# A message-passing layer on one core: the node half of the update moved from the node stage to the end of each group, eight early chunks in place of ten, and early gathers gated on finished table groups

## The reference

```
h   = relu(layernorm(x))                                  # 12500 x 128
m   = relu(concat(h[src], edge_attr) @ msg_w1 + msg_b1)   # 400000 x 128, edge_attr 400000 x 64
msg = m @ msg_w2 + msg_b2
agg = segment_sum(msg, dst)                               # 12500 x 128
u   = relu(concat(h, agg) @ upd_w1 + upd_b1)
out = x + u @ upd_w2 + upd_b2
```

## Time and profile before

| what | value |
|---|---|
| median of three runs | 4690.09 us |
| the profiled execution | 4662.54 us, span 4660.7 us |
| busy: PE, PE weight loads | 2531.2 us, 2175.3 us |
| busy: POOL, DVE, ACT | 2953.8 us, 1924.0 us, 130.3 us |
| granted PE clock, mean | 0.686 of 2.4 GHz |
| HBM | 340.79 MB of packets, 73 GB/s |

### The profile page before, as it was taken

How to read it: one execution, slowest core, us unless ns; L and a number is a source line. 1 busy time by engine, 2 the same in 40 slices (tenths; PEclk the granted TensorE clock), 3 DMA queues, 4 the chain that set the end, 5 groups by cost and what they waited for, 6 DMA issues and landing times.

```text
span 4660.7 us, 32266 instructions
## 1 busy us (share of the span) xinstructions
PE 2531.2 (54%) x10696; PEld 2175.3 (47%) x10696; DVE 1924.0 (41%) x1990; ACT 130.3 (3%) x257; POOL 2953.8 (63%) x3133
## 2 busy tenths in 40 slices
PE   1756555555545555555555455555555555544655
PEld 1655444454444444444444444544444444444554
DVE  1745434344343343443443433434434334344534
ACT  1520000000000000000000000000000000000000
POOL 6265566666666666666666666666666666665665
PEclk6877766666676666666676767667666666666766
DMA  4322222222222222222222222222222222233322
GB/s 112 125 71 73 67 67 72 67 67 72 67 66 72 67 70 68 67 72 67 67 72 67 66 72 67 72 67 67 72 67 66 72 67 70 80 94 86 90 77 59
DMA packets 154626, 340.79 MB, mean 73 GB/s; under 512 B 73895, under 2 KB 74919, under 8 KB 154187
## 3 DMA queue, kind: packets, MB, share of 16 engines
q0 software_dynamic: 100000, 205.00, 16.8%
q1 hardware_dynamic: 46165, 121.97, 8.1%
q10 hardware_dynamic: 8406, 13.14, 0.9%
HBM read 327.06 MB, written 12.81 MB: 73 GB/s over the span
## 4 chain that ended last, share of the span: by engine, by line
issue 40%; PE 24%; POOL 19%; DVE 8%; another core or an unknown queue 6%; DMA 3%; DVEq 0%; ACT 0%; SPq 0%; POOLq 0%
POOL rows L403 19%; PE pre L487 11%; PE seg L540 9%; DVE rows L967 4%; DMA rows<-table,index 3%; DVE h_space L1021 2%; PE seg L458 1%; PE spare L555 1%; PE spare L556 1%; DVE space L1007 0%; PE pre L462 0%; PE spare L585 0%; DVEq L1046 0%; PE pre L508 0%
## 5 line engine op out<-in xcount | busy, mean ns | idle before, releaser
L403 POOL DMA_INDIRECT rows<-table,index x3045 | 2877.1, 945 | 1661.9 <-issue 1091.2
L487 PE MATMUL pre<-w_attr_sb,attrs 128*128 128x256 f32 x3126 | 1339.5, 599 | 1379.6 <-issue 967.4
L487 PEld LDWEIGHTS pre<-w_attr_sb,attrs 128*128 128x128 f32 x3126 | 907.0, 304 | 1663.3 <-issue 1042.2
L967 DVE TENSOR_TENSOR rows<-pre,rows 128x1024 f32<-128x1024 f32 x381 | 465.9, 1223 | 2318.4 <-DMA rows<-table,index 2215.4
L540 PE MATMUL seg<-space,rows 128*128 128x80 f32 x6250 | 965.8, 306 | 547.8 <-issue 547.0
L540 PEld LDWEIGHTS seg<-space,rows 128*128 128x128 f32 x6250 | 988.7, 232 | 560.1 <-issue 513.3
L1087 DVE TENSOR_TENSOR rows<-rows,iota_ps 128x1024 f32<-128x1024 f32 x381 | 464.7, 1220 | 13.1
L1021 DVE TENSOR_REDUCE h_space<-space 128x240 f32<-128x1920 f32 x130 | 438.4, 3373 | 0.0
L1007 DVE TENSOR_TENSOR space<-iota_ps,dst_rel 128x1920 f32<-128x1920 f32 x131 | 280.8, 2144 | 7.3 <-issue 5.9
L787 ACT ACTIVATE h_space<-update 128x500 f32<-128x500 f32 x25 | 27.5, 1101 | 4315.0 <-DVEq L1090 4160.5
L555 PE MATMUL spare<-h_space,w_msg_t_sb 128*128 128x240 f32 (+1 forms) x262 | 112.7, 524 | 6.5 <-issue 4.1
(11 more groups left out here) (77 smaller groups left out, 456.0 us busy)
## 6 DMA issues: line engine op xcount, KB each, us to landing
attrs<-in_attr SPq DMA_DIRECT2D x130, 768.0 KB
rows<-table,index POOLq DMA_INDIRECT x3045
table<-rows SPq DMA_DIRECT2D x20, 224.0 KB
h_space<-in_x ACTq DMA_DIRECT2D x13, 224.0 KB
out<-h_space ACTq DMA_DIRECT2D x13, 224.0 KB
table_first<-in_x ACTq DMA_DIRECT2D x12, 224.0 KB
out<-table_first ACTq DMA_DIRECT2D x12, 224.0 KB
x_all<-in_x SPq DMA_DIRECT2D x2, 1120.0 KB
```

The source lines that it names most:

```text
L403: pool.indirect_dma_start(slot_rows(j)[:, t, :], None, source, bass.IndirectOffsetOnAxis(index[0:EDGES, j, t:t + 1], 0))\
L487: return pe.matmul(columns(j, q, PAIR)[:, two * 2 * D:(two + 1) * 2 * D], attrs[:, j % 2, start:start + EDGES], w_attr_sb[:, :], start=Tru ...
L967: dve.tensor_tensor(hidden, columns(j, q, tiles), hidden, ALU.add).then_inc(summed, 1)
```

## The change

The node half leaves the node stage. `update` is set to zero by ACT instead, in five copies of 2500 columns after its last group. When a group is finished, PE multiplies the group's transposed `h` by `w_node`, adds the group's part of `update` by a product with the identity, both into PSUM, and ACT's relu reads that with the bias. Two early chunks fewer are gathered from `x`, and five of the eight wait for table groups: chunk 3 for group 1, then 5, 9, 12 and 16. The entries of `FIRST_LEADS` are the same.

```diff
-EARLY = 3
-EARLY_CHUNKS = 10
+EARLY = 2
+EARLY_CHUNKS = 8
+
+EARLY_GATES = {3: 1, 4: 5, 5: 9, 6: 12, 7: 16}
...
             for s in range(EARLY_CHUNKS):
                 j, q = divmod(s, PAIRS)
+                if s in EARLY_GATES:
+
+                    pool.wait_ge(table_made, after(EARLY_GATES[s]))
                 gather(x, j, range(q * PAIR, (q + 1) * PAIR))
...
                 last.then_inc(table_ready, 1)
-                pe.wait_ge(update_made, after(g, BACK[k]))
-                pe.matmul(pre[:, k % 2, 512:512 + GROUP], w_node_sb[:, :], h_group(g),
-                          start=True, stop=True).then_inc(update_ready, 1)
...
             def finish_group(g):

+                pe.wait_ge(updates_in, g + 1)
+                need(pe, o_made, g)
+                pe.matmul(spare[:, 0:GROUP], w_node_sb[:, :], h_group(g), start=True, stop=False)
+                pe.matmul(spare[:, 0:GROUP], identity[:, :], update[:, g * GROUP:(g + 1) * GROUP], start=False, stop=True).then_inc(u_summed, 1)
+
                 pe.wait_ge(u_relued, g + 1)
-                need(pe, o_made, g)
...
-            def update_out(g, k):
-
-                act.wait_ge(update_ready, after(g))
-                act.sem_inc(act_turns, 1)
-                act.activation(update[:, bass.ds(g * GROUP, GROUP)], pre[:, k % 2, 512:512 + GROUP], ACT.Identity,
-                               bias=b_upd1_col[:, :]).then_inc(update_made, 1)
...
             node_groups(GBODIES - 1, True)
+
+            act.wait_ge(iota_moved, 1)
+            for g in range(0, GROUPS, UNROLL):
+                last = act.copy(update[:, g * GROUP:(g + UNROLL) * GROUP], iota_ps[:, 0:1].to_broadcast([P, UNROLL * GROUP]))
+            last.then_inc(update_zeroed, 1)
...
-                act.wait_ge(updates_in, g + 1)
-                need(act, o_ready, g)
-                act.activation(u, update[:, g * GROUP:(g + 1) * GROUP].rearrange("f (p r) -> f r p", r=ROWS), ACT.Relu)\
+                act.wait_ge(u_summed, g + 1)
+                act.activation(u, spare[:, 0:GROUP].rearrange("f (p r) -> f r p", r=ROWS), ACT.Relu, bias=b_upd1_col[:, :])\
...
-            dve.wait_ge(update_made, after(GROUPS - 1))
+            dve.wait_ge(update_zeroed, 1)
```

More of the change, by code:

```diff
@@ L207, in gnn_layer @@
         table_ready = sem("table_ready")
-        update_ready = sem("update_ready")
         table_made = sem("table_made")
-        update_made = sem("update_made")
         table_stored = [sem(f"table_stored{k}") for k in range(UNROLL)]
@@ L246, in gnn_layer @@
         early_moved = sem("early_moved")
+        u_summed = sem("u_summed")
         u_relued = sem("u_relued")
+        update_zeroed = sem("update_zeroed")
         o_ready = sem("o_ready")
@@ L629, in early_blocks @@
                             update_sums(0, steps[s - 1][0] - 2)
-                attr_products(0, EARLY, 1)
+                attr_products(0, *divmod(EARLY_CHUNKS, PAIRS))
                 hidden_sums(0, *steps[-1])
-                update_sums(0, EARLY - 2)
-                attr_products(0, EARLY, 2)
+                if steps[-1][1] == 0:
+                    update_sums(0, steps[-1][0] - 2)
+                attr_products(0, *divmod(EARLY_CHUNKS + 1, PAIRS))
             def edge_loops(wide):
@@ L673, in _ @@
             pe.matmul(spare[0:1, 0:EDGES], rel_max[0:EDGES, :], identity[0:EDGES, 0:EDGES], start=True, stop=True).then_inc(rel_max_turned, 1)
-            pe.wait_ge(update_made, after(GROUPS - 1))
+            pe.wait_ge(h_t_made, after(GROUPS - 1))
             pe.wait_ge(span_known, 1)
@@ L688, in _ @@
                 act.dma_start(tile, source).then_inc(w_loaded, 16)
-            for credited in (h_made, update_made, update_ready, h_turned):
+            for credited in (h_made, h_turned):
                 act.sem_inc(credited, CREDIT)
@@ L729, in node_groups @@
                         deviation(i + 1)
-                    update_out(i * UNROLL + k, k)
             deviation(0)
```

## The result

The changed kernel takes 4792.32 us, median of four runs (4780.95 to 4808.06), against 4692.39 for the kernel before beside it: a ratio of 1.0207, 95% interval 1.0164 to 1.025. The forecast was 4738, slower by 48; it is slower by 100. The profiled run took 4780.95 us, with a span of 4779.2, 118.5 over the span before.

What follows compares the result with a forecast made beforehand. POOL's row gathers were taken as the bound, its waits for PE as the rest. Front 9.6, finishing 35 and tail 3 made 48 us on the profiled 4662.54, 4710, lifted to 4738 us; range 4668 to 4795.

Steps and rivals of the forecast that it cites:

- Node stage: First stage, building the table: last table group at T = 120 us, ends 105 and 158, where before it was 182.8.
- Zeroing: ACT's five copies clearing the sums after its last table group: 17 us at most, hidden by 2 us.
- Hand-over: Start of gathers from the table: chunk 8 waits for six hidden sums until T + 72, 192 us, losing the 63 us gain.
- To the ordinary lead: Chunks 8 to 33: 250 us of gathers plus the same 68.5 of waits, chunk 33 at 510.5, 9.6 us later.
- Blocks 12 to 111: Steady edge-stage blocks: the old 34.6 us each, no change forecast.
- The forecast's lift from the profile to the median: Profiled run's forecast of 4710 us raised to 4738, since the three-run median stood 0.6% above the profile.
- Finishing: Blocks 112 to 121, two groups each: 5.2 to 8.8 us more per pair, half on the path, 35 us in all.
- every one of ten blocks like the bad one: Upper end of the finishing term: all ten blocks stall like the one with POOL's 14.78 us wait, 82 us.
- Tail: The last group ends the kernel: 2.0 to 3.8 us more, taken as 3.
- the hidden finish: Rival in the last blocks: the pair's longer chain lies wholly beside the burst, 4703 us, or 4693 with T at 110; chance 0.17.
- The faster rival: Chunks 8 to 33: hidden sums, not gathers, set the start; chunk 33 at 442, 4669 us; chance 0.17.
- The useless gates: Rival in the node stage: gating gathers does not free PE, T = 176, 4794 us; chance 0.08.

Runs made afterwards that it cites:

- the experiment with the lead of 12: Changed kernel with an entry of 12 for block 2 in FIRST_LEADS, so chunk 8 no longer waits for six hidden sums: 4646.29 us, ratio 1.0014 to before.
- the spread kernel: Changed kernel with groups finished one per block from block 104, not two per block from block 112: 4680.03 us, ratio 0.9976 to before.
- the second set: Four kernels on one chip, among them the changed kernel run again unaltered: 4748.68 us, ratio 1.0143 to the kernel before.
- the fourth: Set of single runs on one chip: changed kernel unaltered 4756.74 us, kernel before unaltered twice, 4698.68 and 4681.27 us.
- three kernels of the first: Changed kernel with the old front, with a first lead of 12 for block 2, and without gates: 4679.35, 4646.29 and 4732.16 us.

## Why the prediction was wrong

The direction was right, and 4792 lies in the range; the size was off by half.

- *Node stage.* T (when the last table group is done) = 125.1 against 120: right, and for the reasons given, since it is 154.4 without the gates and 140.9 with the node product left in.
- *Zeroing.* 10.8 us and hidden, as said.
- *Hand-over.* Chunk 8 waited for hidden sums until T + 80, said T + 72; the experiment with the lead of 12 shows it as the front's loss: 45 us in that run, 58 in the spread kernel.
- *To the ordinary lead.* From chunk 8 to 33 the waits were 503.6 - 204.8 - 250 = 49 us, not 68.5. This miss and that of the hand-over cancel in part, so that the front came out near the forecast's +9.6 by luck: +2.7 in these traces, +6 and +11 on another chip, +10.5 between the means.
- *Blocks 12 to 111.* Nothing was forecast and 25 us appear; the same code of before took 3459.1, 3467.3 and 3480.4 there in three traces, and the changed kernel 3471.8 to 3483.7, so most of it belongs to the two executions. The forecast's lift from the profile to the median (0.6%, 28 us) happens to cover such a difference.
- *Finishing: the step that failed.* "Half of a pair's 5 to 9 us on the path, 3.5 us by ten, gives 35". The term was sized as a share of PE's added time at the speed of a quiet stretch. The runs show neither: beside gathers the first answer of a block came after 1.9 to 10.3 us (eleven blocks of the first trace) in place of 1.9, and what counts is when the pair's last sum comes, free if it is 5 us ahead of the burst's end, and later at about a microsecond for each. The term measured 85 in the first traces, 61 in the second set, 45 and 51 in the fourth, and 34 to 45 in three kernels of the first (against before's 433.7 or 428.4). The upper end, "every one of ten blocks like the bad one", 82, is what the first trace did: ten long pauses. With the 25 us of the steady blocks, its 85 make 110 of the 118.5 us between the first two spans. The rows were there: 4175.69 to 4188.03 and the pause of 14.78 are such a pair.
- *Tail.* +5.4 from chunk 372, said 3.

Of the rivals, the hidden finish came true only where one group stood per block. The faster rival failed with chunk 33 at 503.6. The useless gates would have given 4794 us, nearly the measured time, but by another road: their T of 176 did not come. The Trainium skill, page "SBUF — State Buffer", section "Who interferes with whom", says that PE and ACT wait on nobody; by that rule the gates could not help and the products would cost what they cost alone. The runs do not agree: T is 125.1 with the gates and 154.4 without, and two products answered after 1.9 us alone were answered after 8.3 beside gathers. Whether PE waits for anything in SBUF, of which that section speaks, no run shows.

Open: what in the gathers makes PE's answers late (descriptors written by POOL, or the rows arriving), and whether PE works slowly then or only its end is reported late. A lower granted clock is not enough: it takes a product from 1.00 to 1.88 us. Open too is why the number of long pauses differs between executions: seven to ten of eleven in the changed kernel's three traces, two to five in before's three.

## What to carry to other kernels

Work that is hidden under a periodic burst is not priced by its duration but by whether its chain ends before the cover does: look up how far ahead of the burst's end it finishes now, and take durations from beside the burst, not from a quiet stretch. If it doesn't fit, spread the same work over more bursts before making it smaller. When a group of chunks moves to another place, check the lists that are indexed by block: one missing entry was worth 53 us here by the medians. And take two traces of a kernel before subtracting stretches: the hundred steady blocks of the kernel before differed by 0.6% between three executions (3459.1 to 3480.4 us).

## What was not expected of the hardware

Matrix products beside indirect gathers were answered late: two products of 500 columns, 1.9 us by their records, after 8.3 us, and four of 128 columns, 2.07 us by their records, after 7.8 (4201.24 to 4209.03), while without gathers both came within 0.2 us of their modelled ends. No older work of PE stood in front of the four: ACT had the answer to the products before them. Early in a burst the lateness can be absent: in the pair done at 4255.33 the first three answers came within 0.4 us of PE's modelled ends, the last one, 14 us after the first, 5 us late.
